# In the attention kernel's TensorE schedule, projections ahead of the weighted values

## What is computed

```python
q = layernorm(x) @ w_q;  k = ctx @ w_k;  v = ctx @ w_v      # heads of 64
attn = softmax(where(mask, -inf, q @ k.T / 8))
x = x + (attn @ v) @ w_o
x = x + (layernorm(x) @ (int4(kernel) + a @ b) + bias)
```

## Time and profile before

| | us |
|---|---|
| median of three runs | 505.73 |
| lowest and highest | 504.22, 506.14 |
| the profiled execution, its own time | 508.86 |
| its span, first to last instruction | 505.9 |
| PE busy | 451.9 (89%) |
| DVE busy | 405.5 (80%) |
| POOL busy | 399.2 (79%) |
| ACT busy | 327.7 (65%) |

### The profile page before, as it was taken

One profiled execution on the slowest core, in us unless ns is written; L12 is line 12 of the kernel. 1 busy time (PEld: TensorE's weight loads), 2 busy tenths in 40 slices (PEclk: granted clock), 3 DMA queues, 4 the chain that ended last, 5 costly groups with the idle time before them and its releaser, 6 DMA issues.

```text
span 505.9 us, 15465 instructions
## 1 busy us (share of the span) xinstructions
PE 451.9 (89%) x5855; PEld 329.2 (65%) x5855; DVE 405.5 (80%) x1110; ACT 327.7 (65%) x845; POOL 399.2 (79%) x659
## 2 busy tenths in 40 slices
PE   3759679999999999999999999999999999888874
PEld 1425566668666866678666867677767866676652
DVE  4865778989888888889897979888988988887662
ACT  5776655777667756777677765776667766656530
POOL 5495676889888987789787888889787978899941
PEclk9879779999999999999999999999999999999897
DMA  8501576669867996579957996699878786779950
GB/s 291 199 21 32 104 176 99 138 126 201 162 116 146 169 173 126 110 139 196 156 121 145 155 179 135 128 168 188 129 132 140 140 158 135 139 132 173 157 125 26
DMA packets 218817, 71.91 MB, mean 142 GB/s; under 512 B 202785, under 2 KB 216882, under 8 KB 218738
## 3 DMA queue, kind: packets, MB, share of 16 engines
q1 hardware_dynamic: 217680, 69.25, 71.4%
q0 software_dynamic: 480, 1.31, 0.9%
q10 hardware_dynamic: 578, 0.30, 0.2%
HBM read 14.71 MB, written 4.19 MB: 37 GB/s over the span
## 4 chain that ended last, share of the span: by engine, by line
PE 48%; DVE 24%; ACT 14%; POOL 5%; DMA 4%; issue 3%; DVEq 0%; POOLq 0%; ACTq 0%
PE ps_b L907 36%; ACT arena L671 8%; PE ps_a L975 7%; DVE ps_a L800 7%; DMA arena<-arena 3%; DVE arena L793 3%; DVE arena L782 2%; ACT arena L650 2%; PE ps_b L1023 2%; PE ps_b L996 2%; ACT arena L662 1%; DVE arena L748 1%; DVE arena L804 1%; DVE arena L859 1%; POOL arena L583 1%
## 5 line engine op out<-in xcount | busy, mean ns | idle before, releaser
L907 PE MATMUL ps_b<-arena 128*128 128x65 f16 (+3 forms) x3348 | 324.4, 250 | 7.3 <-DVE arena L859 4.0
L907 PEld LDWEIGHTS ps_b<-arena 128*128 128x128 f16 x3348 | 224.9, 99 | 85.1 <-issue 8.7
L671 ACT ACTIVATE arena<-ps_a,arena 128x160 f32<-128x160 f32 x512 | 160.0, 396 | 93.9 <-DVE arena L804 86.3
L583 POOL TENSOR_TENSOR arena<-arena 128x512 f16<-128x512 f32 x128 | 148.3, 1159 | 0.0
L579 POOL CAST arena<-arena 128x512 f16<-128x512 f32 x128 | 78.4, 613 | 55.5 <-ACT arena L671 53.3
L800 DVE TENSOR_REDUCE ps_a<-ps_a 128x4 f32<-128x640 f32 x128 | 105.3, 823 | 0.0
L975 PE MATMUL ps_a<-arena 64*128 64x160 f16 x1536 | 77.1, 234 | 17.2 <-ACT arena L671 17.2
L975 PEld LDWEIGHTS ps_a<-arena 64*128 64x128 f16 x1536 | 51.4, 95 | 41.4 <-issue 20.9
L996 PE MATMUL ps_b<-arena 128*128 128x65 f16 x512 | 72.3, 194 | 0.0
L793 DVE TENSOR_TENSOR arena<-ps_b,arena 128x512 f16<-128x512 f32 x60 | 41.1, 687 | 22.5 <-ACT arena L662 20.5
L859 DVE TENSOR_TENSOR arena<-ps_b,arena 128x256 f32<-128x256 f32 x128 | 54.3, 425 | 4.4
(11 more groups left out here) (139 smaller groups left out, 420.8 us busy)
## 6 DMA issues: line engine op xcount, KB each, us to landing
arena<-in_x_dram SPq DMA_DIRECT2D x8, 512.0 KB
mask_u<-in_x_dram SPq DMA_DIRECT2D x32, 128.0 KB, 2.9
out_dram<-mask_u SPq DMA_DIRECT2D x32, 128.0 KB, 2.7
arena<-arena SPq DMA_TRANSPOSE x128, 3.8
arena<-arena SPq DMA_DIRECT2D x24, 65.0 KB, 2.6
arena<-in_L_xattn_w_q_dram SPq DMA_DIRECT2D x1, 1024.0 KB, 8.7
arena<-in_L_xattn_w_k_dram SPq DMA_DIRECT2D x1, 1024.0 KB, 10.7
arena<-in_L_xattn_w_v_dram SPq DMA_DIRECT2D x1, 1024.0 KB, 12.2
```

The source lines that it names most:

```text
L583: nc.gpsimd.tensor_tensor(lo_main, main, hi_main, ALU.subtract)
L671: ins = nc.scalar.activation(probs[k % 2][:, h, :], p_scores[k % 2][:, h % 2, h // 2 * WINDOW:(h // 2 + 1) * WINDOW], ACT.Exp, bias=neg_ma ...
L907: mm = nc.tensor.matmul(dst, a, c, start=(first and at == 0), stop=(last and at == n - 1))
```

## The change

Only PE's order within a slot changes. In slots 0 to 127 the weighted values move behind the projections and stay ahead of the late work. In the slots from 128 on, which have no scores, they move behind the late work. No instruction is added or removed, and no wait. The order on DVE, ACT, POOL and SP stays the same.

```diff
@@ -1043,12 +1043,14 @@
             def slot(s):
                 if s.k < LAST - 2:
                     scores(s.k + 2)
-                if 0 <= s.k - PV_BEHIND < LAST:
-                    weighted_values(s.k - PV_BEHIND)
                 for i, name in enumerate(s.proj):
                     item(s, i, name)
+                if 0 <= s.k - PV_BEHIND < LAST and s.k < LAST:
+                    weighted_values(s.k - PV_BEHIND)
                 for i, (name, tile) in enumerate(s.late):
                     tail_item(s, len(s.proj) + i, name, tile)
+                if 0 <= s.k - PV_BEHIND < LAST and s.k >= LAST:
+                    weighted_values(s.k - PV_BEHIND)
```

## The result

The changed kernel takes 521.67 us (median of four executions, 521.24 to 523.15), the kernel before, measured beside it, 505.94 us (504.22 to 508.30). The ratio is 1.032, with a 95% interval of 1.029 to 1.035. That is 15.7 us slower. The prediction had the sign and the mechanism of the middle, but its 515.4 us is 6.3 us short, and the time lies outside its range (507 to 519). The profiled execution of after took 521.81 us, with a span of 519.2 us.

What follows compares the result with a forecast made beforehand. It took TensorE (PE, 89% busy) to bound the middle, batches 1 to 6. Batch terms summed to +10.0 us, less 0.3 for the end, +9.7; on 505.73 that gave 515.4 us, range 507 to 519.

Steps and rivals of the forecast that it cites:

- Slots u = 3 to 5: Key-projection slots and the one behind: PE waits for banks that a later DVE releases late; +1.25 us per batch, batches 1 to 6.
- The v chain: Slots 78 to 80: v0 ends earlier on PE, but DVE takes out weighted values first; -0.17 us per batch, batches 0 to 6.
- Slots u = 8 to 12: Query pairs: q5 waits 0.72 us, slot 92's wait goes; net +0.2 us in batches 3 to 5, -0.1 in 1, 0 in 6.
- Batch 2: Holds h, r0 and r1 besides, so more bank waits: +2.3 us more, +3.4 us in all.
- Batch 4: Delay of slots 67 and 68 hides slot 69's DMA wait, -0.4 us; +0.9 us for the batch.
- Batch 0: Other slots (pairs in 7, 11, 12), partly lower clock; estimated from slot 88's steps at +1.0 us, between 0 and 2.
- The end: Slots behind the last scores: PE does f and o0 while awaiting the last transposing DMA; -0.3 us (0 to -1).
- The base: Starting time: profiled execution lies 3.1 us over the median, and the same difference was taken off 518.6, giving 515.4 us.
- A: Rival, key slots: banks are free in time, so no difference; 504 to 507.5 us, chance 0.13.
- B: Rival, value slots: early evacuation wins all 1.08 us of slot 80's stop in 7 batches, -7.6 us; 498 us, chance 0.07.
- C: Rival: new waits in slots 84 and 91 lower the clock, +3 us in 7 batches; 536 us, chance 0.02.
- PE's busy time: Sign in the profile after: PE's busy us would stay about the same, since nothing is added.

Runs made afterwards that it cites:

- e3: Kernel before with the projections ahead of the weighted values only in slots u = 3 and 4 (key pairs); 515.02 us, ratio 1.0166.
- e11: Kernel before with the projections ahead of the weighted values only in slots u = 3; 511.63 us in one execution.
- e7: Changed order on PE in slots 0 to 127 only; on DVE the maxima ahead of taking out the weighted values in slots with projections; 512.66 us, ratio 1.013.
- e1: Kernel before, unchanged, run once more with its own profile; 506.95 us against 506.83, ratio 1.000.
- e14: Kernel before, unchanged, profiled a second time after the first profile and its repeat; 504.61 us.
- e16: Kernel before, unchanged, profiled yet again; 505.87 us.
- e2: Kernel before with the changed order only from slot 128 on; 509.28 us, ratio 1.0055.
- e5: Changed order on PE in slots 0 to 127 only; on DVE the first projection's low part ahead of taking out the weighted values; 543.70 us, ratio 1.074.
- e10: Only the change's first half, projections ahead of weighted values in slots 0 to 127, the order of before from slot 128; 520.10 us against 504.83, ratio 1.0295.
- e6: Kernel before with the weighted values behind a slot's first projection and ahead of its second; from slot 128 on as before; 505.29 us, ratio 0.998.
- e13: Kernel before with the weighted values behind the first projection only in slots u = 5, 12, 14 and 15; 503.00 us against 504.83, ratio 0.9965.
- e17: Changed kernel, unchanged, in its third profile; 523.16 us.
- e15: Changed kernel, unchanged, in its second profile; 522.47 us.

## Why the prediction was wrong in size and right in kind

**Slots u = 3 to 5: right.** Predicted +1.25 us per batch, measured +0.40, +0.75 and +0.11 = +1.26. The single times hit too: slots 83 and 84 7.34 us (7.38 said), reciprocal 3.25 us after the slot's start (3.27), k1 held by 0.37 us (0.39), k3 by 0.50 (0.50). e3 showed it alone, e11 and e7 showed its two causes: the bank of `f` for k1, the late low part of k1 for k3.

**The v chain: right.** Slot 80 is 0.20 us shorter (-0.17 said). v0's low part starts 3.07 us after its slot's start, 3.23 before, directly behind DVE's product. Where e7 puts that low part ahead of the product, it starts at 2.75 us, but slot 80 gains only 0.06 us more, since PE then waits 0.49 us for the product.

**Slots u = 8 to 12: undersized, some 0.2 us a batch.** The wait of q5 was said to cost 0.72 us; it costs 0.53 (slot 91, 3.37 for 2.84). The wait in slot 92 that goes gives back 0.51 us (0.54 said). What the working left out is slots 89 and 93: without projections, they stand right behind a pair whose weighted values ended late, and pay 0.15 us each for DVE's product. I had priced this at the one place where I looked for it, slot 85, and not at the other two. With 0.03 us in each of three more slots the net is +0.41 us, not +0.2. In batch 6, where I said 0, it is the same 0.15 us twice and the small ones.

**Batch 2: undersized.** +3.4 us said, +3.98 measured. `h` is right (slot 37 +0.59 us; 0.1 and 0.6 said). Slots 40, 43 and 44 cost 0.75, 0.59 and 0.75 us, together 2.09, where "0.84 twice" was 1.68; slots 41 and 45 add 0.30.

**Batch 4: near by luck.** +1.07 us (+0.9 said) against the first profile. The -0.4 us counted a wait for a DMA in slot 69, and e1, e14 and e16 don't have that wait (54.8 us for 55.2). Against them batch 4 loses 1.47 us, where the sum without this term gives 1.3. Whether the new order would hide such a wait is not shown.

**Batch 0: the largest miss of one batch.** +1.0 us said. At like clock (before and e1 against after) it is +1.8: slots 8, 12 and 13 cost 0.73, 0.68 and 0.15 us. These are the slots behind and at the pairs of slots 7, 11 and 12, two places of the kind that batch 2 has, and I had taken slot 88's price for the whole. Slots 3 and 4 of batch 0 hold pairs too (k1, x0 and k2, x1), which I had not listed: together they take 7.00 us in each profile of before and 7.24 to 7.36 us in those of the changed kernel. With the clock, the means differ by 2.4 us.

**The end: wrong sign.** -0.3 us said. At like clock (0.82 and 0.83, 0.92 and 0.91) it is +0.3 (20.8 us behind POOL's last split against 20.6, 20.0 against 19.75), because the last weighted values wait behind those of slot 126 on PE and in DVE's taking out, and `o1` waits 1.06 us for them. The `n` of the earlier trace rows is held by ACT for 1.26 us after (1.32 before): that chain has hardly changed. In e2, with the lower clock for longer, it is 2.8 us.

**The base: the largest single step that failed, 3.1 of the 6.3 us.** I took the sum against one profiled execution that lay 3.1 us over the median, and subtracted these 3.1 us from both. But that excess was no constant of the profiling. Against e14 the first profile is 4.3 us longer: 1.2 us in slots 1 to 16 and 0.9 at the end, both with the clock at its lower level for longer, 1.2 until slot 1, 0.5 in slots 17 to 112 and 0.5 behind them. With 9.7 us on its own time the profile gave 518.6 us; the shift to 515.4 assumed that the changed kernel's median would lose the same 3.1 us. It did not: its median, 521.67 us, is that of its profiled execution, 521.81. It kept the low stretch of batch 0 in all three profiles and had one more in slot 113.

**The prices: the other half, 3.2 us.** The profiled execution took 521.81 us where the sum gave 518.6. Slots 1 to 112 of the first two profiles differ by 12.6 us, where the batches of the sum give 10.0, and the end has 0.6 us more than said. (The low stretch in slot 113, +1.6 us, and a start that was 1.2 us shorter nearly cancel in this pair.) With the right prices and the same base the forecast would have been 518.6 us, still 3.1 short.

**Rivals.** A (the banks are free) failed: PE waits for banks in slots 83, 84 and 91. B's gain, the stop in slot 80, was 0.20 us of 1.08. C, the clock, was put at all or nothing: every batch at +3 us, chance 0.02. From 125 to 394 us of the changed kernel it was indeed 1.00 throughout, with stops of 0.2 to 0.4 us. But it did act at the rims, worth some 3 us, which my cases had nowhere. Of the signs, one failed: PE's busy time was to stay about the same and rose by 8.9 us, for the reason given with slots 83 and 84 and at the lower clock of the rims. The Trainium skill's "TensorE: Matmul & The Clock Gate", section "A second HAM failure mode: psum-queue depth-cycling", says that frequent short idles between matmul groups can make the clock swing. The changed kernel's middle doesn't bear that out (clock 1.00 over 268 us). e5's slot 81 is in keeping with it in batches 4, 5 and 6, where `w` runs at the lower level behind waits of 0.34 and 0.98 us, and not in batches 2 and 3, with the same waits and the full clock.

**What stays open.** Why the clock falls at the rims. That the order bears on it is likely: the drop in slot 113 is in eight profiles of nine with the order changed in most slots and in one of nine without. But it can't be in every execution: e10 has three of six at a mean clock of 0.974, which are 2 us shorter and were not profiled. By what the order does it is open, since PE's wait ahead of the drop is the same in all. The loss of e2 is open in the same way. The new low stretch is therefore seen to cost some 1.6 us, but its cause is not shown. SP's new wait for the weighted values (line 501, 7.8 us in ten places, 2.2 at most) was not tested by itself; in the slots read here the waits of PE and DVE account for the lengths without it.

## What to carry to other kernels

When work is put behind other work on one engine, its reader on the next engine becomes late, and so does everything that this reader's fixed list has behind it; list each user of that list, the slots without the moved work too, and price it once per slot, not once per kind. A short piece that separates two users of rotating banks can be worth more than the wait it causes itself. Here, between the two projections, it lost at most some 0.2 us in a slot of the middle (e6, slots 20 and 29) and won where the wait had been, slot 92 (e6, e13); behind both it cost most. And before a profiled execution is used as a base, find out why it differs from the median: here that was the clock at the rims, which the changed kernel didn't share.

## What the runs showed of the hardware

The kernel before takes 503.5 to 510.0 us from execution to execution, and the profiles put this spread into a few places: the start (slot 1 at 49.7 to 49.8 or at 51.0 us), the first slots of batch 0 and the last 70 us, where PE has real gaps. In the last two the granted clock falls to 1.2 GHz, or stays there longer, in some executions and not in others. That costs 1.2 to 1.5 us in slots 1 to 16 (58.6 or 57.1 to 57.3 us) and 1.5 to 1.7 us in slot 113 (`w` 2.79 or 4.41 us). A fall in slot 121 makes that slot as much longer (5.16 us in e16, 5.39 in e17, 3.73 in the other profiles of the two kernels), but the time to POOL's last split isn't longer for it: 44.0 us in e16 as in before, 45.7 us in e17 as in e15. A single stop isn't enough to bring the clock down: it stays full behind 1.08 to 1.26 us in e5 and behind 1.62 us in nine of the 17 profiles that have that wait. A change worth 0.5% has to be read from the length of the batches at full clock, which repeats to 0.1 us a batch (but for the one late DMA), and not from the total alone: e6 and e13 are alike in the middle to 0.1 us, and their ratios are 0.998 and 0.9965, with the low stretch of slot 113 in the profile of e6 and not in that of e13.
